# Another slot plan for the first batch of an attention and mixture kernel: maxima, stores, ropes, resident weights

## The chip, the cores and the metric

One core of a Trainium2 chip runs the whole program. The metric is the device time of one execution in microseconds, as the median of several runs. Smaller is better. The compute engines are TensorE (PE in the rows), VectorE (DVE), ScalarE (ACT) and GpSimd (POOL); SyncE (SP) only issues transfers here.

## The reference, cut to what matters

For four batches of 512 tokens with 512 channels:

```python
xn = layernorm(x)
q = rope(rms_norm(xn, q_norm_w))            # 16 heads of 32
k = rope(rms_norm(ctx, k_norm_w)); v = ctx  # 4 heads of 32, each for 4 query heads
x = x + (causal softmax(q k / sqrt(32)) v) @ w_out.T
xt = layernorm(x)
probs = softmax(xt @ w_router)              # 128 experts, the 4 largest kept
basis = silu(xt @ w_gate) * (xt @ w_up)     # 8 units of 256
x = x + sum over the kept experts of coeff * (mix of basis) @ w_down
      + (silu(xt @ shared_w_gate) * (xt @ shared_w_up)) @ shared_w_down
```

## The kernel before

**Precision.** Products are made from high and low parts: a copy into the rounded type is the high half, the original minus it the low half. A product of weights is three matmuls: high by high, high by low, low by high. So every weight chunk in use has to be split first: the high half on ScalarE (`weights_high`, L931), the low one on VectorE (`weights_low`, L1260) for three of the four row blocks and on GpSimd (L889) for the fourth. The router's weights and `w_down` stay in SBUF and are split once: `resident_high` on ScalarE (L933) and `resident_low` on VectorE (L1263), in slot 36. `mixture_table` (L1244), six small instructions on VectorE, stands in slot 32.

**Slots.** There is one time axis of slots, from -40 to 247. Each engine's program is a loop over the slots; in each it asks a fixed list of questions ("is there a tile to turn here?") and emits what is due, with semaphore waits for its inputs. So tables of slot numbers at the top of the file set each engine's order. An engine never overtakes in its own list, and neither does SyncE's queue of transfers.

**Attention.** A batch is cut in two halves of 256 queries; a half has five tiles: tile 0 (5, 10, ...) the keys, the other four the queries of one key head each. A tile is roped (tiles 0 to 2 on VectorE, the others on GpSimd, first part in its slot, rest in the next), turned by TensorE (L1443), copied out as a high half by ScalarE (`turned_high`, L945) and a low half by VectorE (L1181), and then stacked by DMAs into `k_st` or `q_st`, three for each query head (L679). Tile 5 goes through DRAM: it is stored by two DMAs (L649), waited for, and loaded back by three for each of two pairs of heads (L669). The two halves of a turned tile lie in `turned_h` and `turned_l`, which have two places each, by even and odd tile: tile 6 has to wait until tile 4's copies have read theirs. One span u is a key head in a half; u 0 to 3 is the first half of the first batch, 4 to 7 the second. A span is scored in eight matmuls (L1483), each with a row maximum on VectorE (L1203) and a sum of exponentials on ScalarE (L965). In spans 0 to 3 these exponentials are themselves turned (L1494, out of the bank by L981 on ScalarE). From span 4 on the row maxima are split (L1212, L1214), turned (`maxima_turn`, L1463), copied (`maxima_out`, L957) and sent to `q_st` by two DMAs (L687), and the scores are made a second time, transposed (L1507), with their exponential (L983). Values follow (L1522), and the output's high and low halves (L988, L855).

**Short banks.** Three PSUM banks serve scores, turns, maxima, inverses, router products and x turns in rotation, in the order in which `short_products` lists them; each product waits for the reader of the third before it.

**Mixture.** From slot 32 on (`START`) a token pair each 24 slots: projection and residual (slots 32 and 33 for the first), x turns (35 and 37, L1531), router (38 and 39, L1542), then units of two 512-wide products (from 40, L1607), and the shared and down products. Chunk 0 (`w_out`) is used in slot 32, chunk 1 in 40, chunk 2 in 44, chunk 3 in 46; `SPLIT` puts their high halves 3 and 2 slots before, the low ones 2 and 1. The loads of chunks 0 to 2 and of the resident weights are issued in the first 15 us.

Of the kernel before, what the change touches and what calls it, by code (L numbers as in the profile page):

```python
# [16 lines left out]
LEAD = dict(inverse=-1, spread=2, second_pass=4, inverse_turn=5, values=(9, None), high=0)  # L17

FIRST_TILES = dict(
    rope=(-34, -32, -20, -12, -7, 6, 9, 16, 23, 27), turn=(-17, -13, -8, -1, 6, 12, 15, 21, 27, 34),  # L20
    stack=((), (), (), (), (7,) * 4, (13,) * 2, (16,) * 4, (22,) * 4, (28,) * 4, (35,) * 4))
# [9 lines left out]
THROUGH_DRAM = (5,)  # L31
ROPE_DVE = (0, 1, 2)
# [39 lines left out]
def attention_and_mixture_kernel(nc, x, ctx_in, q_norm_w, k_norm_w, w_out, w_router, w_units, w_down,  # L72
# [48 lines left out]
    with common:  # L121
# [437 lines left out]
        def short_products(s):  # L559
# [11 lines left out]
            if (u := of_later_span(s, "maxima")) is not None:  # L571
                found.append(("maxima", u - KV))
# [60 lines left out]
        def sync_engine(e):  # L633
# [12 lines left out]
            def store_turned(n):  # L646
                for i, (part, made) in enumerate(((turned_h, s_th), (turned_l, s_tl))):
                    e.wait_ge(made, n + 1)
                    e.dma_start(turned_copy[n, i].rearrange("d j q -> j d q"), f32(part[:, n % 2, :])).then_inc(s_stored[n % 2][i], 16)  # L649

            def stack_keys(n, i):
# [7 lines left out]
                if not through_dram(n):  # L659
                    e.wait_ge(s_tl, n + 1)  # L660
                    for head in range(2):
                        for row, part in rows:
                            e.dma_start(f32(k_st[row:row + D, c % KR + head, h * Q:(h + 1) * Q]),
                                        f32((turned_h, turned_l)[part][(j + head) * D:(j + head + 1) * D, n % 2, :])
# [7 lines left out]
            def stack_queries(n, j):  # L672
# [5 lines left out]
                for row, part in ((D, turned_h), (2 * D, turned_h), (0, turned_l)):  # L678
                    e.dma_start(f32(q_st[row:row + D, u % QR, j, :]),  # L679
                                f32(part[j * D:(j + 1) * D, n % 2, :])).then_inc(s_q[u % QR][j], 16)  # L680
# [247 lines left out]
        def scalar_engine(e):  # L928
# [4 lines left out]
            def resident_high():  # L933
                e.wait_ge(s_rt, 16)
                e.activation(rt_w[:, :, 0:NE], rt_raw[:, :, NE:2 * NE], ACT.Copy).then_inc(s_rth, 1)
                e.wait_ge(s_wd, 16)
                for k in range(KD):
                    e.activation(wd_h[:, k, :], wd_raw[:, k, :], ACT.Copy).then_inc(s_wdh, 1)

            def turned_high(n):  # L940
                e.wait_ge(s_turn, n + 1)
                if n - 2 > U0:
                    for s, v in turned_read(n - 2):
                        e.wait_ge(s, v)
                e.activation(turned_h[:, n % 2, :], short("turn", n)[:, 0:Q], ACT.Copy).then_inc(s_th, 1)  # L945
# [104 lines left out]
            for s in slots:  # L1050
                for u in attended_before(s):
# [13 lines left out]
                if s == START[0] + 4:  # L1065
                    resident_high()
# [4 lines left out]
                if (u := of_later_span(s, "maxima")) is not None:  # L1071
# [676 lines left out]
```

## Time and profile before

| | |
|---|---|
| median of 3 runs | 821.03 us (819.33 to 822.58) |
| profiled execution, its own time | 823.38 us |
| its span, first to last instruction | 821.6 us |
| mean granted TensorE clock | 0.979 |
| busy: TensorE / VectorE / ScalarE / GpSimd | 94 / 79 / 70 / 65 % |

The page divides the span in 40 slices; TensorE is under 90% busy in the first six of them and at 90% or more from the seventh on, except the last. Its clock is below full in the third, fourth and fifth. Times in the rows are from the start of the span.

### The profile page before, as it was taken

Reading aid. Unit: us, or ns where it says so; the run is one execution under the profiler, and the core shown is the slowest. Engines: PE = TensorE matmul, PEld = TensorE weight load, DVE = VectorE, ACT = ScalarE, POOL = GpSimd, SP = SyncE. Lnnn points to the kernel's source line nnn. Section 1 sums busy time; section 2 is a strip of 40 time slices with the busy share of each in tenths; the row PEclk is TensorE's granted clock in tenths of the full one; section 3 lists DMA queues with packets and bytes.
Section 4 is the critical chain, followed back from the end, with each engine's and each line's share of the span. In section 5 each row is a group of like instructions: output and inputs, shape, how many; then the busy total and the mean of one; then the engine's idle time right before and its main releaser. Section 6 shows DMA issues by size and latency. Waiting matters only on the chain. (4 is left out here: it accounts for less than half of the span.)

```text
span 821.6 us, 15292 instructions
## 1 busy us (share of the span) xinstructions
PE 771.2 (94%) x4180; PEld 613.0 (75%) x4180; DVE 649.0 (79%) x1635; ACT 576.9 (70%) x1413; POOL 531.3 (65%) x685
## 2 busy tenths in 40 slices
PE   2768689999999999999999999999999999999998
PEld 2645467787778778787778788877778887788876
DVE  6656787888898787888798796888788887688774
ACT  3867877787778677787778677787777775654542
POOL 5546669876577858877477868867465615652561
PEclk9957899999999999999999999999999999999999
DMA  8321225554555445754545445554545345444550
GB/s 294 112 66 34 81 82 174 165 165 149 182 170 173 129 144 178 239 180 135 197 160 164 149 131 181 174 167 156 185 154 177 129 131 197 161 155 156 199 183 26
DMA packets 57053, 127.03 MB, mean 155 GB/s; under 512 B 10921, under 2 KB 28041, under 8 KB 56969
## 3 DMA queue, kind: packets, MB, share of 16 engines
q1 hardware_dynamic: 56968, 126.04, 46.5%
q8 instruction: 36, 0.59, 0.3%
q14 instruction: 49, 0.39, 0.2%
HBM read 107.55 MB, written 4.46 MB: 136 GB/s over the span
## 5 line engine op out<-in xcount | busy, mean ns | idle before, releaser
L1607 PE MATMUL u<-w_h,t_h 128*128 128x512 f32 x640 | 258.1, 403 | 4.3 <-issue 1.9
L1607 PE MATMUL u<-w_l,t_h 128*128 128x512 f32 x640 | 250.4, 391 | 0.0
L1607 PE MATMUL u<-w_h,t_l 128*128 128x512 f32 x640 | 250.3, 391 | 0.0
L1260 DVE TENSOR_TENSOR w_l<-w_raw,w_h 128x512 fp32r<-128x512 f32 x288 | 244.1, 875 | 0.2 <-ACT w_h L931 0.2
L931 ACT ACTIVATE w_h<-w_raw 128x512 fp32r<-128x512 f32 x384 | 219.0, 621 | 11.8 <-DMA w_raw<-in_w_units 11.7
L889 POOL TENSOR_TENSOR w_l<-w_raw,w_h 128x512 fp32r<-128x512 f32 x96 | 138.8, 1445 | 101.8 <-ACT w_h L931 101.6
L965 ACT ACTIVATE scores<-scores,mx 128x384 f32<-128x384 f32 (+1 forms) x224 | 128.8, 575 | 76.0 <-DVE mx L1203 74.6
L897 POOL TENSOR_TENSOR macc<-macc,gb 128x256 f32<-128x256 f32 x112 | 106.2, 952 | 63.9 <-DVE gb L1363 63.5
L1203 DVE CUSTOM_DVE_ANT_0 scores<-s,mask_qk 128x384 f32<-128x384 f32 (+1 forms) x224 | 112.5, 503 | 42.1 <-PE s L1483 41.1
L1607 PEld LDWEIGHTS u<-w_h,t_h 128*128 128x128 f32 x640 | 120.6, 188 | 30.5 <-issue 7.0
L1607 PEld LDWEIGHTS u<-w_h,t_l 128*128 128x128 f32 x640 | 120.1, 188 | 26.9
L1607 PEld LDWEIGHTS u<-w_l,t_h 128*128 128x128 f32 x640 | 120.8, 189 | 19.9
L1483 PE MATMUL s<-k_st,q_st 96*128 96x384 f32 (+1 forms) x248 | 89.5, 373 | 6.6 <-DMA q_st<-turned_l 3.4
L1342 DVE SCALAR_TENSOR_TENSOR th<-th,u 128x256 f32<-128x256 f32 x160 | 66.5, 416 | 36.0 <-ACT th L1030 34.7
L983 ACT ACTIVATE pr<-pair 128x1024 f32<-128x1024 f32 x88 | 77.6, 882 | 20.7 <-PE pair L1507 20.5
L1030 ACT ACTIVATE th<-u 128x256 f32<-128x256 f32 x160 | 60.1, 376 | 36.9 <-PE u L1607 36.5
L872 POOL TENSOR_SCALAR_AFFINE_SELECT pr<-pr 128x512 f32<-128x512 f32 x56 | 46.1, 824 | 36.7 <-ACT pr L983 36.7
L1363 DVE SCALAR_TENSOR_TENSOR gb<-th,wt,u 128x256 f32<-128x256 f32 x112 | 53.9, 481 | 16.0
L1483 PEld LDWEIGHTS s<-k_st,q_st 96*128 96x128 f32 x248 | 49.4, 204 | 19.8 <-issue 11.5
L1507 PE MATMUL pair<-q_st,k_st 98*128 98x512 f32 x148 | 52.5, 422 | 0.9 <-ACT pr L983 0.9
L965 ACT ACTIVATION_READ_ACCUMULATOR scores<-scores,mx 128x1 f32 x224 | 42.5, 190 | 0.0
L1522 PE MATMUL o_bank<-pr,ct 128*32 128x256 f32 (+1 forms) x768 | 42.5, 362 | 0.0
(150 smaller groups left out, 1188.1 us busy)
## 6 DMA issues: line engine op xcount, KB each, us to landing
w_raw<-in_w_units SPq DMA_DIRECT2D x160, 512.0 KB, 4.2
w_raw<-in_w_out_t SPq DMA_DIRECT2D x16, 512.0 KB, 4.7
w_raw<-in_shared_w_down SPq DMA_DIRECT2D x16, 512.0 KB, 4.6
q_st<-turned_h SPq DMA_DIRECT2D x232, 32.0 KB, 2.8
out<-x SPq DMA_DIRECT2D x16, 256.0 KB, 2.1
q_st<-turned_l SPq DMA_DIRECT2D x116, 32.0 KB, 2.6
x<-in_x SPq DMA_DIRECT2D x3, 1024.0 KB, 8.8
k_st<-turned_h SPq DMA_DIRECT2D x48, 32.0 KB, 2.8
```

Source lines behind the costliest of these rows:

```text
L889: e.tensor_tensor(w_l[:, i % WR, k, :], w_raw[:, i % WR, k, :], f32(w_h[:, i % WR, k, :]), ALU.subtract).then_inc(s_wlp, 1)
L897: e.tensor_tensor(total, total, gb[:, adds_before(w, g) % 2, :], ALU.add).then_inc(s_acc, 1)
L931: e.activation(w_h[:, i % WR, k, :], w_raw[:, i % WR, k, :], ACT.Copy).then_inc(s_wh, 1)
L965: e.activation(s, s, ACT.Exp, bias=mx[:, u % 2, t, j:j + 1], scale=-1.0, accum_out=sums[:, u % 2, t, j:j + 1]).then_inc(s_sum, 1)
L983: e.activation(pr[:, n % PR, 0:width], pair[:, 0:width], ACT.Exp, scale=-1.0).then_inc(s_ex, 1)
L1030: e.activation(th[:, n % 2, :], u_bank[filler_no[f] % 2][:, 0:I], ACT.Tanh, scale=0.5).then_inc(s_tanh, 1)
L1203: e.tensor_tensor_reduce(masked_scores(u, m), scores_bank(i)[:, 0:width], mask_qk[:, T - width:T], 1.0, 3e38, ALU.add, ALU.min, mx[:, u % ...
L1260: e.tensor_tensor(w_l[:, i % WR, k, :], w_raw[:, i % WR, k, :], f32(w_h[:, i % WR, k, :]), ALU.subtract).then_inc(s_wl, 1)
L1342: e.scalar_tensor_tensor(th[:, n % 2, :], th[:, n % 2, :], 1.0, up, ALU.add, ALU.mult).then_inc(s_ga, 1)
L1363: e.scalar_tensor_tensor(to, th[:, n % 2, :], scale, gate_v, ALU.mult, ALU.mult).then_inc(s_gb, 1)
L1483: e.matmul(scores_bank(i)[:, 0:w], q_st[0:MAXROW, u % QR, j, t * P:(t + 1) * P], k_st[0:MAXROW, (b * KV + kv) % KR, 0:w], start=True, stop ...
L1607: last = e.matmul(u_bank[n % 2][:], t[:, k, cols], ww[:, i % WR, k, :], start=(k == 0 and m == 0), stop=(k == KC - 1 and m == 2))
```

## The change

It moves work between slots in the first batch and changes who does part of it:

- `FIRST_TILES`: the ropes of tiles 6 to 9 go from slots 9, 16, 23, 27 to 8, 14, 19, 24; the second moments from slot 7 to 5, the query scale from 9 to 7, the spreading of the inverse by one slot.
- Stacking: the fourth query head of tile 4 is copied in slot 13, behind the stores of tile 5 (slot 12); tile 6's first head (16) goes ahead of the first key pair of tile 5 (17); then two heads of tile 6 (18), the second key pair and the last head (19).
- `OWN_PLACE`: tile 6's halves lie in the first columns of `t_h` and `t_l`, the buffers of the turned x, which are first used in slot 35; the first x turn's copy waits for tile 6's copies.
- For spans 4 to 7 the turn of the maxima and its copy stand ahead of the tile turn in their slot, on TensorE, on ScalarE and in the order of the short banks (`maxima_in`).
- The resident weights are split wholly by VectorE, one of six steps in each of slots 12, 13, 14, 15, 16 and 18, the copies with `tensor_copy`; the table of the mixture is in slot 19.
- `FIRST_SPLIT`: chunk 0's halves in slots 15 to 18, chunk 1's in 29 to 31, chunk 2's in 37 to 39.

```diff
-LEAD = dict(inverse=-1, spread=2, second_pass=4, inverse_turn=5, values=(9, None), high=0)
+LEAD = dict(inverse=-1, spread=1, second_pass=4, inverse_turn=5, values=(9, None), high=0)
 FIRST_TILES = dict(
-    rope=(-34, -32, -20, -12, -7, 6, 9, 16, 23, 27), turn=(-17, -13, -8, -1, 6, 12, 15, 21, 27, 34),
-    stack=((), (), (), (), (7,) * 4, (13,) * 2, (16,) * 4, (22,) * 4, (28,) * 4, (35,) * 4))
+    rope=(-34, -32, -20, -12, -7, 6, 8, 14, 19, 24), turn=(-17, -13, -8, -1, 6, 12, 15, 21, 27, 34),
+    stack=((), (), (), (), (7, 7, 7, 13), (17, 19), (16, 18, 18, 19), (22,) * 4, (28,) * 4, (35,) * 4))
...
+OWN_PLACE = 6
...
-PREP = dict(key_squares=(-39, 4, -29, -10), key_scale=(-36, 5, -26, -7), query_scale=(-35, 9, -23, -6))
+PREP = dict(key_squares=(-39, 4, -29, -10), key_scale=(-36, 5, -26, -7), query_scale=(-35, 7, -23, -6))
 SPLIT = dict(high=(3, 2), low=(2, 1))
-MOMENTS = (-39, -38, 4, 7, -32, -27, -13, -9)
+FIRST_SPLIT = dict(high=((15, 17), (29, 30), (37, 38)), low=((16, 18), (30, 31), (38, 39)))
+RESIDENT, MIX_TABLE = (12, 13, 14, 15, 16, 18), 19
+MOMENTS = (-39, -38, 4, 5, -32, -27, -13, -9)
...
+        def maxima_in(s, first):
+            u = of_later_span(s, "maxima")
+            return u if u is not None and (u < H * KV) == first else None
...
         def splits(s, name):
-            return [(i, k) for i, at in enumerate(chunk_slot) for ks, ahead in zip(((0, 1), (2, 3)), SPLIT[name])
-                    if s == at - ahead for k in ks]
+            found = []
+            for i, at in enumerate(chunk_slot):
+                early = FIRST_SPLIT[name]
+                places = early[i] if i < len(early) else [at - ahead for ahead in SPLIT[name]]
+                found += [(i, k) for ks, place in zip(((0, 1), (2, 3)), places) if s == place for k in ks]
+            return found
...
+        def turned(n):
+            return (t_h[:, 0, 0:Q], t_l[:, 0, 0:Q]) if n == OWN_PLACE else (turned_h[:, n % 2, :], turned_l[:, n % 2, :])
...
             found += [("scores", u * G * TH + m) for u, m in first_pass_tiles(s)[:1] if not apart(u * G * TH + m)]
+            if (u := maxima_in(s, first=True)) is not None:
+                found.append(("maxima", u - KV))
             for n in tiles_in(s, "turn"):
...
-            def resident_high():
-                e.wait_ge(s_rt, 16)
-                e.activation(rt_w[:, :, 0:NE], rt_raw[:, :, NE:2 * NE], ACT.Copy).then_inc(s_rth, 1)
-                e.wait_ge(s_wd, 16)
-                for k in range(KD):
-                    e.activation(wd_h[:, k, :], wd_raw[:, k, :], ACT.Copy).then_inc(s_wdh, 1)
...
             def turned_high(n):
                 e.wait_ge(s_turn, n + 1)
-                if n - 2 > U0:
-                    for s, v in turned_read(n - 2):
+                for m in [m for m in range(U0 + 1, n) if m % 2 == n % 2 and OWN_PLACE not in (m, n)][-1:]:
+                    for s, v in turned_read(m):
                         e.wait_ge(s, v)
-                e.activation(turned_h[:, n % 2, :], short("turn", n)[:, 0:Q], ACT.Copy).then_inc(s_th, 1)
+                e.activation(turned(n)[0], short("turn", n)[:, 0:Q], ACT.Copy).then_inc(s_th, 1)
...
+                elif g == 0:
+                    for s, v in turned_read(OWN_PLACE):
+                        e.wait_ge(s, v)
...
-            def resident_low():
-                e.wait_ge(s_rth, 1)
-                e.tensor_tensor(rt_w[:, :, NE:2 * NE], rt_raw[:, :, NE:2 * NE], f32(rt_w[:, :, 0:NE]), ALU.subtract).then_inc(s_rtl, 1)
-                for k in range(KD):
+            def resident_weights(step):
+                if step == 0:
+                    e.wait_ge(s_rt, 16)
+                    e.tensor_copy(rt_w[:, :, 0:NE], rt_raw[:, :, NE:2 * NE]).then_inc(s_rth, 1)
+                elif step == 1:
+                    e.wait_ge(s_rth, 1)
+                    e.tensor_tensor(rt_w[:, :, NE:2 * NE], rt_raw[:, :, NE:2 * NE], f32(rt_w[:, :, 0:NE]), ALU.subtract
+                                    ).then_inc(s_rtl, 1)
+                elif step < 2 + KD:
+                    k = step - 2
+                    e.wait_ge(s_wd, 16)
+                    e.tensor_copy(wd_h[:, k, :], wd_raw[:, k, :]).then_inc(s_wdh, 1)
+                else:
+                    k = step - 2 - KD
                     e.wait_ge(s_wdh, k + 1)
-                    e.tensor_tensor(wd_l[:, k, :], wd_raw[:, k, :], f32(wd_h[:, k, :]), ALU.subtract
-                                    ).then_inc(s_wdl, 1)
+                    e.tensor_tensor(wd_l[:, k, :], wd_raw[:, k, :], f32(wd_h[:, k, :]), ALU.subtract).then_inc(s_wdl, 1)
...
-                if s == START[0]:
-                    mixture_table()
-                if s == START[0] + 4:
-                    resident_low()
...
+                if s in RESIDENT:
+                    resident_weights(RESIDENT.index(s))
+                if s == MIX_TABLE:
+                    mixture_table()
```

In `store_turned`, `stack_keys`, `stack_queries` and `turned_low` the operands come from `turned(n)`; the loops of ScalarE and TensorE ask `maxima_in(s, first=True)` at the head of the slot, or behind the first scores, and `first=False` where they asked before.

## Rows read from the trace of the kernel before

**Rows 1.** Windows: stretch, its length, busy us (instructions) by engine, clock, DMA share, GB/s.
```profile
36.00:53.80 17.80, 10.32 (x65) 7.84 (x61) 7.27 (x38) 11.74 (x40) 11.27 (x22) 0.69 0.26 68
...
117.00:821.60 704.60, 694.24 (x3775) 556.66 (x3773) 568.86 (x1375) 499.38 (x1213) 466.54 (x564) 1.00 0.49 161
```

**Rows 2.** TensorE's waits from 50 to 120 us: us in total, times, longest.
```profile
PE s L1531 <- DVE mx L1203: 3.8, 2, 2.0
PE s L1483 <- DMA q_st<-turned_l: 3.4, 2, 3.1
PE s L1443 <- POOL r_b L849: 1.9, 2, 1.0
PE u L1607 <- DVE w_l L1260: 1.4, 2, 0.8
...
PE s L1463 <- DVE mhl L1214: 1.0, 1, 1.0
PE pair L1507 <- ACT pr L983: 0.9, 1, 0.9
...
PE u L1591 <- POOL o_l L855: 0.5, 1, 0.5
```

**Rows 3.** Timeline, TensorE: start us, us, instruction, idle before it and releaser.
```profile
53.82 0.66 PE L1483 MATMUL s<-k_st,q_st 96*128 96x384 f32 x1 [3.06 <-DMA q_st<-turned_l]
...
85.03 0.63 PE L1531 MATMUL s<-ident,xn 128*128 128x128 f32 x4 [1.79 <-DVE mx L1203]
...
91.61 1.08 PE L1531 MATMUL s<-ident,xn 128*128 128x128 f32 x4 [1.98 <-DVE mx L1203]
```

**Rows 4.** Timeline, the queue of SyncE.
```profile
34.83 1.24 SPq L679 DMA_DIRECT2D q_st<-turned_h  x2
...
43.72 0.64 SPq L649 DMA_DIRECT2D turned_copy<-turned_h  x1
...
47.16 3.13 SPq L669 DMA_DIRECT2D k_st<-turned_copy  x6
50.39 1.22 SPq L679 DMA_DIRECT2D q_st<-turned_h  x2
```

**Rows 5.** Timeline, VectorE; first its group of low halves from the page.
```profile
L1260 DVE TENSOR_TENSOR w_l<-w_raw,w_h 128x512 fp32r<-128x512 f32 x288 | 244.1, 875 | 0.2 <-ACT w_h L931 0.2
...
40.35 0.42 DVE L1181 TENSOR_TENSOR turned_l<-s,turned_h 128x256 fp32r<-128x256 f32 x1 [1.27 <-ACT turned_h L945]
...
46.50 0.28 DVE L1203 CUSTOM_DVE_ANT_0 early<-u,mask_qk 128x128 f32<-128x128 f32 x1
...
54.52 0.56 DVE L1203 CUSTOM_DVE_ANT_0 scores<-s,mask_qk 128x384 f32<-128x384 f32 x1 [2.37 <-PE s L1483]
...
73.11 0.78 DVE L1246 TENSOR_TENSOR amp<-amp 128x16 f32<-128x16 f32 x1
...
74.71 0.29 DVE L1256 TENSOR_SCALAR mixs<-amp_s,es 128x8 f32<-128x8 f32 x1
...
88.61 0.85 DVE L1265 TENSOR_TENSOR rt_w<-rt_raw,rt_w 128x512 fp32r<-128x512 f32 x1 [0.99 <-ACT rt_w L935]
89.38 1.28 DVE L1268 TENSOR_TENSOR wd_l<-wd_raw,wd_h 128x512 fp32r<-128x512 f32 x2
...
99.44 1.23 DVE L1212 TENSOR_SCALAR mhl<-mx 128x8 fp32r<-128x8 f32 x1
```

**Rows 6.** Timeline, ScalarE.
```profile
45.07 0.38 ACT L945 ACTIVATE turned_h<-s 128x256 fp32r<-128x256 f32 x1 [1.52 <-DMA q_st<-turned_l]
...
48.31 1.00 ACT L981 ACTIVATE pr<-pair 128x1024 f32<-128x1024 f32 x1
...
68.59 1.13 ACT L931 ACTIVATE w_h<-w_raw 128x512 fp32r<-128x512 f32 x2
```

**Rows 7.** Timeline, GpSimd.
```profile
42.59 0.72 POOL L849 TENSOR_TENSOR r_b<-r_b 128x256 f32<-128x256 f32 x1
...
99.37 1.27 POOL L889 TENSOR_TENSOR w_l<-w_raw,w_h 128x512 fp32r<-128x512 f32 x1 [2.59 <-ACT w_h L931]
```

More of the change, by code:

```diff
@@ L570, in short_products @@
             found += [("scores", u * G * TH + m) for u, m in first_pass_tiles(s)[1:] if not apart(u * G * TH + m)]
-            if (u := of_later_span(s, "maxima")) is not None:
+            if (u := maxima_in(s, first=False)) is not None:
                 found.append(("maxima", u - KV))
@@ L646, in store_turned @@
             def store_turned(n):
-                for i, (part, made) in enumerate(((turned_h, s_th), (turned_l, s_tl))):
+                for i, (part, made) in enumerate(zip(turned(n), (s_th, s_tl))):
                     e.wait_ge(made, n + 1)
-                    e.dma_start(turned_copy[n, i].rearrange("d j q -> j d q"), f32(part[:, n % 2, :])).then_inc(s_stored[n % 2][i], 16)
+                    e.dma_start(turned_copy[n, i].rearrange("d j q -> j d q"), f32(part)).then_inc(s_stored[n % 2][i], 16)
             def stack_keys(n, i):
@@ L663, in stack_keys @@
                             e.dma_start(f32(k_st[row:row + D, c % KR + head, h * Q:(h + 1) * Q]),
-                                        f32((turned_h, turned_l)[part][(j + head) * D:(j + head + 1) * D, n % 2, :])
+                                        f32(turned(n)[part][(j + head) * D:(j + head + 1) * D, :])
                                         ).then_inc(s_k[c // 2 % (KR // 2)][h], 16)
@@ L677, in stack_queries @@
                 e.wait_ge(s_tl, n + 1)
-                for row, part in ((D, turned_h), (2 * D, turned_h), (0, turned_l)):
+                for row, part in ((D, 0), (2 * D, 0), (0, 1)):
                     e.dma_start(f32(q_st[row:row + D, u % QR, j, :]),
-                                f32(part[j * D:(j + 1) * D, n % 2, :])).then_inc(s_q[u % QR][j], 16)
+                                f32(turned(n)[part][j * D:(j + 1) * D, :])).then_inc(s_q[u % QR][j], 16)
             def rows(u):
@@ L1050, in scalar_engine @@
             for s in slots:
+                if (u := maxima_in(s, first=True)) is not None:
+                    maxima_out(u)
                 for u in attended_before(s):
@@ L1064, in scalar_engine @@
                     x_high(g)
-                if s == START[0] + 4:
-                    resident_high()
                 if (p := routing(s, "choose")) is not None:
@@ L1070, in scalar_engine @@
                     row_sum(u, m)
-                if (u := of_later_span(s, "maxima")) is not None:
+                if (u := maxima_in(s, first=False)) is not None:
                     maxima_out(u)
@@ L1180, in turned_low @@
                 e.wait_ge(s_th, n + 1)
-                e.tensor_tensor(turned_l[:, n % 2, :], short("turn", n)[:, 0:Q], f32(turned_h[:, n % 2, :]), ALU.subtract
+                high, low = turned(n)
+                e.tensor_tensor(low, short("turn", n)[:, 0:Q], f32(high), ALU.subtract
                                 ).then_inc(s_tl, 1)
@@ L1389, in vector_engine @@
                     evict[fillers[s - 1][0]](fillers[s - 1])
-                if s == START[0]:
-                    mixture_table()
-                if s == START[0] + 4:
-                    resident_low()
                 for u, m in first_pass_tiles(s)[1:]:
@@ L1652, in tensor_engine @@
                     pass_a(u, m)
+                if (u := maxima_in(s, first=True)) is not None:
+                    maxima_turn(u)
                 for n in tiles_in(s, "turn"):
@@ L1660, in tensor_engine @@
                     pass_a(u, m)
-                if (u := of_later_span(s, "maxima")) is not None:
+                if (u := maxima_in(s, first=False)) is not None:
                     maxima_turn(u)
```

## The prediction

> **What bounds the kernel now.** The page's busy shares put TensorE first of the engines. The windows by stretch, read next, show where it is not busy: from 117 us to the end it is busy 694.2 of 704.6 us, with the clock granted at 1.00, while between 36 and 53.8 us it is busy 10.3 of 17.8, at a mean clock of 0.69, so that part of this stretch runs at the lower of the two levels, 1.2 GHz instead of 2.4 [rows 1]. Every engine works through a list whose order is fixed by slots. What TensorE gains before 117 us is therefore kept: the rest is its own work and moves forward as a block. What the change does in slots 5 to 45 is to be read from who releases TensorE there. The table of its waits from 50 to 120 us names them: VectorE's row maxima 3.8 us, a query DMA 3.4, the rope tiles of GpSimd 1.9, low weight halves 1.4, the split maxima 1.0, the second exponential 0.9, the low half of the attention output 0.5 [rows 2]. The timeline gives the place of each.
>
> **The clock of the slots.** By order and shape of the instructions, TensorE's 53.82 us in [rows 3] is slot 21, the first scores of the second half (span 4); 85.03 is the first x turn in slot 35, 91.61 the second x turn in slot 37. 72 us is slot 32, 101 us slot 40 and 117 us slot 45.
>
> **Part 1, the stores and copies.** SyncE issues tile 4's twelve copies from 34.83 on, then makes the two stores of tile 5 from 43.72 on, waits for the landing, loads the keys from 47.16 and starts tile 6's queries only at 50.39 [rows 4]; TensorE stands at 53.82 for them, 3.06 us [rows 3]. In the new order three of tile 4's copies go behind the store. One head is three issues, about 1.9 us (six took 3.13 [rows 4]), so the store goes out near 41.8, and the moved head by 44.9. Tile 6's first head needs its low half, which was there some 0.8 us after ScalarE's high half began at 45.07. That had waited 1.52 us for tile 4's copies to leave the buffer [rows 6]; in a place of its own tile 6 does not, and I put its low half at 45.2. It is issued by 47.0, the two key heads by 48.8. Before, the first head's last issue ended near 50.39 + 1.9 = 52.3 and TensorE went on at 53.82, 1.5 later [rows 3, 4]; so all is there at about 50.3, with 1 us of doubt. The DMA wait is gone. Cover for the later heads is thin: the fourth is issued by 56 us and needed near 60.
>
> What is late next? The resident weights, chunk 0 and the table of the mixture are put in just this stretch. **VectorE** in slots 12 to 18 gets three copies, three subtractions and chunk 0's three subtractions, and in slot 19 the table. Subtractions of this size take 1.28 us for two [rows 5], so I take 0.6 apiece. A copy of this shape on VectorE isn't in the trace; half of that, 0.3, is one end, and 0.6 plus the wait below is the other, and I take 0.6, since the operand is as long. Before slot 17's row maximum stand seven of these nine, 4.2 us. The engine was idle there for some 3.3 us between the tile-5 low half at 40.35 and that maximum at 46.50 [rows 5], of which tile 6's shorter wait takes back about 0.6. So the maximum comes at 48.3 to 48.5. **ScalarE** waits for it, then has the two high halves that are new in slot 17, 1.13 us for two, and only then the sum and the exponential that began at 48.31 [rows 6]: now 50.6. TensorE's next turning of probabilities needs it out of its bank. Before, TensorE stood at slot 21 from 53.82 - 3.06 = 50.76 on [rows 3], 2.45 us after that exponential's start; so it comes to slot 21 at about 53.1. Also the table, 1.9 us from 73.11 to 75.00 [rows 5], now stands before the last maximum of slot 20. VectorE's first maximum of the second half, 54.52 before [rows 5], comes at 53.5 to 54.2. I book 1.0 us of the 3.4; bounds are -1.5 (each of nine operations 0.3 dearer than taken) and +3.4 (all hidden).
>
> On GpSimd's side the trace shows a VectorE instruction of 8 elements a partition that took 1.23 us from 99.44; it ended when the subtraction on GpSimd that had begun at 99.37 and lasted 1.27 us ended [rows 5, 7]. So a neighbour on GpSimd can hold a small one-source operation for its whole length. Tile 7's rope now runs in slots 14 and 15, beside those copies. It speaks against moving copies to VectorE, and rival (c) has its price. The Trainium skill states it as a rule (SBUF — State Buffer, section "SBUF: two separate sides"): a VectorE operation in a two-port mode, or one with two SBUF inputs, and a GpSimd operation exclude each other for a whole instruction. The row at 99.44 agrees.
>
> **Part 2, ropes sooner.** GpSimd made tile 6 last at 42.59 to 43.31 [rows 7], behind an output half that waits for the values of span 0. With the second moments in slot 5, the scales in slot 7 and the first part in slot 8 it ends near 41.6. That only feeds tile 6's turn, which stands before the chain counted above: no gain of its own. Tiles 8 and 9 are made in slots 19 and 24 instead of 23 and 27, where GpSimd had been idle. Tile 8's turn then doesn't wait, about half of the 1.9 us for ropes, 0.9 [rows 2]. The other half is tile 10's, in the second batch, whose chain starts at the first residual and isn't touched. The maxima of span 4 wait for their split, which stands on VectorE behind tile 8's low half, and move with it: this is the same 0.9 us, not a second one. GpSimd is then also free when the output half for the first projection is due: 0.5 us [rows 2], against nothing if ScalarE's half comes no sooner; I take it whole. Sum 1.4.
>
> **Part 3, the maxima sooner.** The maxima now stand ahead of the turn in the order of the three short banks too, so that each short product waits for another reader. In slot 35 the x turn waited for the maximum of its third predecessor; this now is a low half, up to 1.79 us earlier [rows 3]. But the scores right behind it (6.3) take over the same wait, by which they start at most 0.5 us sooner, and behind them tile 10's rope holds. Gain zero, bound 0.5. In slots 28, 34 and 40 the rows of the maxima go out to the queue 1 to 3 us sooner; no wait for them is in the table, so I book nothing. In slot 40 the maxima wait for the logits in the turn's place (1.1 us, which stays).
>
> **Part 4, the resident weights out of slot 36.** VectorE spent 88.61 to about 90.6 on three subtractions [rows 5], and behind them came the maximum that the second x turn awaited until 91.61, 1.98 us [rows 3]. Without them the maximum comes 2 us sooner, and the x turn starts where TensorE had begun to wait, at 91.61 - 1.98 = 89.6. It had run at 1.2 GHz, too: 1.08 us for four transposes, where the first x turn took 0.63 [rows 3]. Behind it ScalarE is busy nearly without a gap until 101 us, so the shift is passed on. I book 2.3 of 2.0 to 2.6.
>
> **Part 5, chunks 1 and 2 sooner.** Chunk 2's halves leave slots 41 to 43 for 37 to 39, where chunk 1's had been, and chunk 1's take chunk 0's old slots. The loads had long landed. So slots 29 to 31 and 37 to 39 have the same amount as before, and 41 to 43 have less by three subtractions on VectorE. TensorE's two waits for low weights, 1.4 us, and the wait on an exponential, 0.9 us [rows 2], whose maximum stood behind them, go: 2.3 us. From below it is bounded by 1.0, if the next chunk (issued to the queue in slot 34, used in 46) or SyncE's long line of copies is late next.
>
> **Sum.** 1.0 + 1.4 + 0 + 2.3 + 2.3 = 7.0 us. The profiled run took 823.38 us for its span of 821.6, the median is 821.03; so the span would be 814.6, such a profiled run 816.4, and against the median the forecast is 814.0.
>
> **Rivals.**
> (a) Everything early is hidden and the clock helps. If copies cost 0.3 and the chain in slots 12 to 20 stays under TensorE's own slow work, all 3.4 us of the DMA wait are won, 2.4 more; and with fewer gaps before 66 us the clock may not fall there, for which I put 1.0 of TensorE's work that runs slowly today. 7.0 + 3.4 = 10.4, so 810.6. For it: VectorE is busy only 7.3 of 17.8 us between 36 and 53.8 [rows 1]. Against it: the operations stand in front of maxima, in the same queue.
> (b) The early chain costs its lower bound, -1.5 in place of 1.0, and part 5 gives 1.0 in place of 2.3: 7.0 - 2.5 - 1.3 = 3.2, so 817.8. For it: ScalarE has 11.7 of 17.8 us there already [rows 1] and gets two more. This is also the case in which the DMA order does not help at all, since TensorE is late anyway.
> (c) Slower: VectorE and GpSimd hold each other. The nine operations and the table's first, ten, each wait a full neighbour as the one at 99.44 did. That instruction's excess is at least 1.1 us over one of a few hundred ns, and 10 x 1.1 = 11, all on the chain of slots 12 to 20: 821.0 - 7.0 + 11 = 825.0. It turns the change slower from 0.7 us apiece. Against it: the 288 low halves of the whole run, beside a GpSimd in all states, took 875 ns in the mean against 640 for those at 89.38, an excess of 0.24 [rows 5].
>
> **How the numbers follow.** The forecast has 0.46, with 811.5 to 816.5 as its own range; (a) 0.18, (b) 0.26, (c) 0.10. The range of 809 to 820 leaves out most of (c) and the best of (a). Half a per cent, 4.1 us, is about what a measurement of this kernel can tell. Faster by more is under 816.9: nearly all of the forecast and (a) and a little of (b), 0.66. Within it: most of (b) and some of (c), 0.26. Slower: 0.08.
>
> **What the profile after would show.** Part 1: no wait for a query DMA at slot 21, keys issued before 49 us; and TensorE at slot 21 at about 53, with ScalarE's sum of slot 18 behind two high halves. If slot 21 begins near 51, (a) is right; at 54 or later, (b) or (c). VectorE's copies: 0.3 or 0.6 us, and above 1 us beside GpSimd for (c). Part 2: no rope wait at tile 8. Part 4: the second x turn 1.5 to 2 us sooner after tile 10's turn. Part 5: no low-weight waits in slot 44. TensorE should reach its unbroken stretch near 110 us instead of 117; the busy 694 us behind it should stay. What would make all of it wrong is a fall of the clock in a place where it now is 1.00, or a wait in slots 44 to 50 that today hides behind those that go.

## The result and the profile after

The changed kernel takes 815.57 us in the median (814.18 to 816.52, six runs), the kernel before 820.86 beside it: a ratio of 0.9937, 95% interval 0.9921 to 0.9952, so 5.2 us less. A second comparison gave 0.9950 (experiment 1). The profiled execution took 816.52 us for a span of 814.8. That of before lay 2.5 us above its median and this one 0.95 above its own, so the two traces show 6.9 us of difference where the medians show 5.2. The other 1.7 us come from which executions were profiled, and not from the change.

TensorE is at 94% of the span as before, VectorE up from 79 to 80. Windows by stretch (stretch, its length, busy us and instructions of TensorE, its weight loads, VectorE, ScalarE, GpSimd; clock, DMA share, GB/s):

```profile
36.00:53.80 17.80, 10.21 (x56) 7.57 (x54) 13.17 (x42) 12.41 (x38) 16.21 (x24) 0.67 0.26 72
66.00:82.00 16.00, 14.06 (x64) 9.98 (x56) 10.28 (x30) 12.81 (x29) 7.18 (x14) 0.79 0.26 83
82.00:100.00 18.00, 14.10 (x82) 9.43 (x83) 12.50 (x35) 15.18 (x38) 12.48 (x23) 0.81 0.15 43
117.00:814.80 697.80, 687.55 (x3743) 551.23 (x3741) 565.07 (x1361) 493.03 (x1198) 460.61 (x558) 1.00 0.49 162
```

The late stretch is as full as it was: 687.6 of 697.8 us, against the row in [rows 1]. What changed lies ahead of it. In 36 to 53.8 us VectorE went from 7.3 busy us to 13.2 and GpSimd from 11.3 to 16.2, and TensorE has about the same (10.2 against 10.3). Its waits from 50 to 120 us, to be read against [rows 2]:

```profile
PE pair L1518 <- ACT pr L991: 4.6, 2, 3.1
PE s L1507 <- DVE mx L1217: 3.7, 3, 2.0
...
PE u L1615 <- POOL o_l L872: 0.4, 1, 0.4
```

The 3.4 us for a query DMA, the rope waits, the 3.8 at the x turns and the 1.4 for low weights are no longer in the table. (In the trace of experiment 1, the same kernel at a fuller clock, one rope wait of 1.3 us is there again.) In the place of the first stands a wait on ScalarE's exponential of up to 3.1 us, and one on VectorE's maximum of 2.0. TensorE's timeline gives the places:

```profile
51.02 1.09 PE L1518 MATMUL pair<-ident,early 128*128 128x128 f32 x4 [3.07 <-ACT pr L991]
52.11 0.52 PE L1507 MATMUL s<-k_st,q_st 96*128 96x384 f32 x1
55.48 1.10 PE L1507 MATMUL s<-k_st,q_st 96*128 96x384 f32 x2 [1.99 <-DVE mx L1217]
...
80.18 0.66 PE L1555 MATMUL s<-ident,xn 128*128 128x128 f32 x4
82.22 0.47 PE L1507 MATMUL s<-k_st,q_st 96*128 96x512 f32 x1 [1.39 <-DVE mx L1217]
...
86.80 0.63 PE L1555 MATMUL s<-ident,xn 128*128 128x128 f32 x4
```

Slot 21 (96x384 at 52.11) has no wait of its own any more and begins 1.7 us sooner than the 53.82 of [rows 3], but two waits of 3.07 and 1.99 us stand around it. The x turns start at 80.18 and 86.80 without a wait (85.03 and 91.61 in [rows 3]).

Two traces need not start alike. The third of TensorE's early groups of transposes stands ahead of all that was changed, and so serves as a mark; first before, then after:

```profile
19.01 1.94 PE L1455 MATMUL u<-ident,r 128*96 128x128 f32 x8 [2.67 <-DVE r L1177]
18.80 1.94 PE L1479 MATMUL u<-ident,r 128*96 128x128 f32 x8 [2.67 <-DVE r L1190]
```

### The profile page after: what moved, and what is told of

It is laid out like the page before. It is cut to its first block and busy times, and to the rows that moved or that the text cites. A ratio compares the mean times of both kernels' runs of the same rounds, so it can differ in the third digit from the quotient of the medians.

```text
span 814.8 us, 15292 instructions
## 1 busy us (share of the span) xinstructions
PE 768.0 (94%) x4180; PEld 610.7 (75%) x4180; DVE 651.2 (80%) x1638; ACT 576.1 (71%) x1410; POOL 531.6 (65%) x685
```

## The experiments

All times below as "us under before" are (1 - ratio) times the median of the kernel before in the same session: 820.43 (experiments 1 to 4), 819.88 (5 to 8), 820.55 (9 to 12).

**1. The changed kernel again.** No edit.

> The changed kernel once more, as the yardstick for its neighbours on the same chip. All theories: 5 to 6 us under the kernel before (ratio 0.993).

Ratio 0.9950, 0.9934 to 0.9966: 4.1 us under before. Its profiled run has the clock at 1.00 from 82 to 100 us where the first one had 0.81:

```profile
82.00:100.00 18.00, 12.54 (x80) 9.16 (x73) 13.59 (x38) 15.53 (x39) 12.84 (x24) 1.00 0.13 35
```

Nearly the same instructions, another clock, and a span of 812.0 instead of 814.8. Of the 2.8 us, 1.0 was there before the clocks differed: the mark stands at 17.83 instead of 18.80, and from it to the third score of the second half both traces take 36.7 us.

```profile
17.83 1.94 PE L1479 MATMUL u<-ident,r 128*96 128x128 f32 x8 [2.68 <-DVE r L1190]
```

So a single trace says where an engine waits, but its total is no measure of a variant to 2 us.

**2. The order alone.** Parts 1 to 3 stay; the resident weights go back to ScalarE and slot 36, the table to 32, all chunks to their old slots.

```diff
-FIRST_SPLIT = dict(high=((15, 17), (29, 30), (37, 38)), low=((16, 18), (30, 31), (38, 39)))
-RESIDENT, MIX_TABLE = (12, 13, 14, 15, 16, 18), 19
+FIRST_SPLIT = dict(high=(), low=())
+RESIDENT, MIX_TABLE = (12, 13, 14, 15, 16, 18), 32
...
+                if s == START[0] + 4:
+                    resident_high()
...
+                if s == START[0] + 4:
+                    for step in (1, 4, 5):
+                        resident_weights(step)
```

The first of these stands on ScalarE, the three subtractions on VectorE; `RESIDENT` itself is no longer asked.

> The changed kernel's stores, copies, ropes, own place and maxima, but resident weights, table and chunk splits where they were before. Theory 1 (the weights' work in slots 12 to 19 takes the place of the DMA wait): without that work the 3.4 us of the wait are really won, and 1.4 at tile 8 and the first projection; 4 to 5 us faster than before, slot 21's third score near 52.5 us. Rival 2 (something else than that work is late next, so the new order of copies brings nothing): 1 to 2 us faster.

0.9945 (0.9929 to 0.9962), 4.5 us under before, as expected. That is as much as the whole change gives. Slot 21 begins at 49.96, 3.9 us sooner than before, but not without a wait: with VectorE and ScalarE relieved, the keys' loads come last, and they are there close to the 50.3 us at which the prediction had put them.

```profile
49.96 0.42 PE L1517 MATMUL s<-k_st,q_st 96*128 96x384 f32 x1 [1.54 <-DMA k_st<-turned_copy]
```

From 36 to 120 us TensorE waits 5.1 us for stacked keys and queries here. So the new order moves SyncE's queue forward, and in the changed kernel the early work of the other engines hides what is left of it.

**3. The weights alone.** Parts 4 and 5 stay; tiles, stores, ropes and maxima are as before.

```diff
-OWN_PLACE = 6
+OWN_PLACE = None
...
-            return u if u is not None and (u < H * KV) == first else None
+            return u if u is not None and (u < 0) == first else None
```
(and the old lists of ropes, stacks, moments, scale and spread)

> The kernel before with the resident weights, the table and the chunk splits moved, everything else as before. Theory 1: the early work hides under the old DMA wait at slot 21, and the gains at slots 37 and 44 remain: 4 to 5 us faster. With order_only the sum of the two is 8 to 10 and the changed kernel's 5.3 is less than that sum. Rival 2: the early work costs in both kernels, 2 to 3 us faster, and the two parts add up to 5.3.

0.9978 (0.9964 to 0.9993), 1.8 us, under the 4 to 5 of the first theory and just under the 2 to 3 of the rival. TensorE's timeline around slot 21:

```profile
52.20 0.63 PE L1515 MATMUL pair<-ident,early 128*128 128x128 f32 x4 [3.21 <-ACT pr L991]
53.42 0.66 PE L1504 MATMUL s<-k_st,q_st 96*128 96x384 f32 x1 [0.45 <-DMA q_st<-turned_l]
```

The query DMA of [rows 3], unmoved in this kernel, is still awaited, but for 0.45 us instead of 3.06: TensorE now comes late by itself, held 3.21 us by the exponential. The new chain on VectorE and ScalarE fills the old wait to the brim, but delays nothing behind it: the first projection starts at 72.20, before it was 72.03. With the DMA's wait also removed (the full change) the chain takes its place. So the 1.8 us are what parts 4 and 5 bring with an early chain that costs nothing here.

**4. The order and the chunks, with the resident weights late.** All of the change, but the router's weights and the table in slot 32 and `w_down` in 58 to 61.

```diff
-RESIDENT, MIX_TABLE = (12, 13, 14, 15, 16, 18), 19
+RESIDENT, MIX_TABLE = (32, 32, 58, 59, 60, 61), 32
```

(and the loop that emits the steps, so that two may share a slot)

> The changed kernel with the six steps of the resident weights and the table moved to where VectorE waits: router steps and table in slot 32, w_down's in slots 58 to 61 (it is first needed in slot 66). Chunk 0's halves stay in slots 15 to 18. Theory 1: the VectorE chain of slots 12 to 19 is shorter by some 7 us of work, slot 21 starts 1.5 to 2.5 us sooner, and the total is 7 to 8 us under the kernel before. Rival 3 (ScalarE's two high halves of chunk 0 in slot 17 make the delay, not VectorE's): as the changed kernel, 5 to 6 us.

0.9914 (0.9894 to 0.9933), 7.1 us under before and 3 under the changed kernel in the same session, as the first theory said. VectorE and ScalarE:

```profile
44.53 1.67 DVE L1274 TENSOR_TENSOR w_l<-w_raw,w_h 128x512 fp32r<-128x512 f32 x2
...
52.18 0.56 DVE L1217 CUSTOM_DVE_ANT_0 scores<-s,mask_qk 128x384 f32<-128x384 f32 x1
```
```profile
48.38 1.00 ACT L991 ACTIVATE pr<-pair 128x1024 f32<-128x1024 f32 x1
```

The exponential begins 1.5 us sooner than after's 49.87 and the first maximum of the second half 2.6 sooner than its 54.77. Slot 21 begins at 50.62, 1.5 sooner. TensorE still waits 2.9 us for that exponential (to 49.52), which stands behind chunk 0's high halves as well.

**5 to 7. The three parts of the order, one at a time.** Before, with only the stack lists and `OWN_PLACE`; only the ropes, moments, scale and spread; only `maxima_in`.

```diff
-    stack=(..., (7,) * 4, (13,) * 2, (16,) * 4, ...)
+    stack=(..., (7, 7, 7, 13), (17, 19), (16, 18, 18, 19), ...)     # 5: with OWN_PLACE = 6
...
-    rope=(-34, -32, -20, -12, -7, 6, 9, 16, 23, 27)
+    rope=(-34, -32, -20, -12, -7, 6, 8, 14, 19, 24)                 # 6
...
+            if (u := maxima_in(s, first=True)) is not None:           # 7
+                maxima_turn(u)
```

> The kernel before with the new order of stores and copies and tile 6's own place, nothing else. Theory 1 (the DMA wait at slot 21 was a real 3.4 us): 2 to 3.5 us faster than before, less than the full wait because tile 6's rope still comes at 43.3 us. Rival 2 (only the order together with the ropes does it): within 1 us.

0.9966 (0.9951 to 0.9981), 2.8 us, as expected. No DMA is among TensorE's waits from 36 to 120 us. The ropes (3.4 us) and the maxima at the x turns (3.4) are first in the table now; in the same window of the kernel before they had 3.0 and 3.8, so neither has taken the DMA's place. The wait for low weights, with the chunks where they were before, is half of the 1.4 in [rows 2]:

```profile
PE u L1641 <- DVE w_l L1283: 0.7, 1, 0.7
```

> The kernel before with only the ropes, second moments, query scales and inverse spreads sooner. Theory 1: 1.4 us faster (tile 8's rope wait and the output half for the first projection), the DMA wait stays. Rival 2: nothing, as the shift at slot 27 goes to SyncE's queue.

0.9989 (0.9975 to 1.0002), 0.9 us, which the interval does not hold apart from nothing. The DMA wait that the stores would have removed is there as before:

```profile
PE s L1514 <- DMA q_st<-turned_l: 3.4, 2, 3.0
```

> The kernel before with only the maxima of spans 4 to 7 turned and copied sooner. Theory 1: within 0.5 us of before, since no wait for their rows stood in the table. Rival 4 (the other readers that the bank rotation gives each product cost or save something at the x turns): 1 us or more, either way.

1.0002 (0.9990 to 1.0013): nothing. The table of waits shows that it did act: of two waits at the x turns, 3.8 us in [rows 2], one is left. The time is the same, so what the turn gained was lost behind it, as part 3 of the prediction argued.

```profile
PE s L1562 <- DVE mx L1223: 2.0, 1, 2.0
```

The three add to 2.8 + 0.9 - 0.2 = 3.5 us against 4.5 together. The intervals of the four (about 1.2 us each way) leave open whether together they are worth more.

**8. The order, resident weights late, chunks unmoved.**

```diff
-FIRST_SPLIT = dict(high=((15, 17), (29, 30), (37, 38)), low=((16, 18), (30, 31), (38, 39)))
-RESIDENT, MIX_TABLE = (12, 13, 14, 15, 16, 18), 19
+FIRST_SPLIT = dict(high=(), low=())
+RESIDENT, MIX_TABLE = (32, 32, 58, 59, 60, 61), 32
```

> resident_late with the chunk splits of before (chunk 0 in slots 29 to 31, 1 in 37 to 39, 2 in 41 to 43). Theory 1: part 4's 2.3 us on top of order_only's 4.6, about 813.5, and the chunk moves are worth about 1 us beside resident_late. Rival 3 (chunk 0's halves in slots 15 to 18 cost as much as chunk 2's departure from slots 41 to 43 brings): the same 812.5 as resident_late or less.

0.9936 (0.9919 to 0.9953), 5.3 us, only 0.7 more than the order alone and less than expected. TensorE's table of waits, 36 to 120 us, has a DMA in it: the rows of the maxima, which stand in SyncE's queue behind the copies of the tiles.

```profile
PE pair L1532 <- DMA q_st<-m_t: 2.5, 1, 2.5
```

**9. The order with the chunks moved, resident weights in slot 36.** The edit of experiment 2 without its `FIRST_SPLIT`.

> The changed kernel with only the resident weights and the table put back (slots 36 and 32); the chunk splits stay moved. Theory 1 (the early VectorE work costs as much as slot 36 gives back): within 1 us of the changed kernel, ratio 0.9935 to 0.996. Rival 5 (taking the resident weights out of slot 36 is worth the 2.3 us booked even net of its early cost): 2 us slower than the changed kernel, 0.997.

0.9930 (0.9917 to 0.9943), 5.7 us, 1.2 more than the order alone, which the intervals do not resolve. It lies near the first theory (0.9935 to 0.996) and far from the rival's 0.997.

**10. The order with the resident weights early, chunks unmoved.** The changed kernel with `FIRST_SPLIT = dict(high=(), low=())`.

> The changed kernel with the chunk splits of before (resident weights and table stay in slots 12 to 19). Against order_resident_late (0.9936) it has the VectorE work in slots 12 to 19 instead of 32 and 58 to 61 and nothing else differs. Theory 1: 2 to 3.5 us slower than that, 0.9965 to 0.998. Rival 3 (the early cost is chunk 0's alone): equal to it, 0.9936.

0.9918 (0.9902 to 0.9935), 6.7 us. Both expectations missed: the kernel is not slower than with the resident weights late (experiment 8) but 1.4 us faster, which the intervals do not resolve. The early resident weights by themselves bring 2.2 us over the order alone, about what part 4 booked without any cost. VectorE, ScalarE and TensorE:

```profile
45.26 0.68 DVE L1293 TENSOR_TENSOR wd_l<-wd_raw,wd_h 128x512 fp32r<-128x512 f32 x1
45.86 0.28 DVE L1217 CUSTOM_DVE_ANT_0 early<-u,mask_qk 128x128 f32<-128x128 f32 x1
...
46.41 0.81 DVE L1293 TENSOR_TENSOR wd_l<-wd_raw,wd_h 128x512 fp32r<-128x512 f32 x1
...
51.60 0.56 DVE L1217 CUSTOM_DVE_ANT_0 scores<-s,mask_qk 128x384 f32<-128x384 f32 x1
```
```profile
47.32 1.02 ACT L991 ACTIVATE pr<-pair 128x1024 f32<-128x1024 f32 x1
```
```profile
65.69 1.22 PE L1531 MATMUL pair<-q_st,k_st 98*128 98x512 f32 x2 [1.55 <-DMA q_st<-m_t]
```

The maximum of slot 17 comes at 45.86, the exponential at 47.32 and the first maximum of the second half at 51.60: all sooner than with the resident weights late but chunk 0 moved (experiment 4).

**11. All of the change, resident weights late, and the second half of chunk 0 two slots later** (the low halves of its first half one slot later).

```diff
-FIRST_SPLIT = dict(high=((15, 17), (29, 30), (37, 38)), low=((16, 18), (30, 31), (38, 39)))
-RESIDENT, MIX_TABLE = (12, 13, 14, 15, 16, 18), 19
+FIRST_SPLIT = dict(high=((15, 19), (29, 30), (37, 38)), low=((17, 20), (30, 31), (38, 39)))
+RESIDENT, MIX_TABLE = (32, 32, 58, 59, 60, 61), 32
```

> resident_late with chunk 0's second high halves behind slot 19's exponential instead of ahead of slot 18's, and its low halves in slots 17 and 20. Theory 1 (two high halves on ScalarE stand in the chain of slots 17 to 20 for 1.1 us): about 1 us faster than resident_late, 811.5, if SyncE's queue does not take it. Rival 6 (from resident_late on SyncE's queue of copies is the bound of slots 21 to 31): the same 812.5.

0.9907 (0.9895 to 0.9920), 7.6 us, the fastest of all, though with four runs only and not resolved from experiment 4, so neither theory is decided. The exponential that began at 48.38 there comes at 46.51, 1.9 us sooner than there, and TensorE's third score still waits for a maximum, and its transposed scores for the rows:

```profile
52.92 1.10 PE L1508 MATMUL s<-k_st,q_st 96*128 96x384 f32 x2 [1.85 <-DVE mx L1217]
...
65.85 0.74 PE L1532 MATMUL pair<-q_st,k_st 98*128 98x512 f32 x2 [1.16 <-DMA q_st<-m_t]
```

**12. Tile 7's rope out of the crowded slots.** The changed kernel with that rope in 17 instead of 14, to take GpSimd's two passes away from VectorE's copies.

```diff
-    rope=(-34, -32, -20, -12, -7, 6, 8, 14, 19, 24)
+    rope=(-34, -32, -20, -12, -7, 6, 8, 17, 19, 24)
```

> The changed kernel with tile 7's rope in slots 17 and 18 instead of 14 and 15, so that VectorE's copies in slots 14 and 15 and chunk 0's first low halves have no rope beside them on GpSimd. Theory 1 with contention (each operation beside GpSimd pays 0.2 to 1 us): 1 us faster than the changed kernel in the end and w_l in slot 16 at 1.28 us for two instead of 1.55. Rival 7 (the contention only moves to slots 17 and 18): the same within 0.7 us.

0.9940 (0.9926 to 0.9954), the same as the changed kernel. The contention moved elsewhere, as the rival said: VectorE's low halves of the chunk came down to 1.28 us for two, and `w_down`'s took 1.22 each where 0.69 is usual, the first beside the output's low half (GpSimd, 45.32 to 46.58), the second beside the rope (48.55 to 49.70).

```profile
44.71 1.28 DVE L1274 TENSOR_TENSOR w_l<-w_raw,w_h 128x512 fp32r<-128x512 f32 x2
45.91 1.22 DVE L1293 TENSOR_TENSOR wd_l<-wd_raw,wd_h 128x512 fp32r<-128x512 f32 x1
49.03 1.22 DVE L1293 TENSOR_TENSOR wd_l<-wd_raw,wd_h 128x512 fp32r<-128x512 f32 x1
```

**The kernels with the new order, side by side** (us under before):

| resident weights | chunks unmoved | chunks moved | moved, chunk 0 partly later |
|---|---|---|---|
| slot 36 | 4.5 (exp. 2) | 5.7 (9) | |
| early, 12 to 18 | 6.7 (10) | 5.2 and 4.1 (the change; 1) | |
| late, 32 and 58 to 61 | 5.3 (8) | 7.1 (4) | 7.6 (11) |

Going down the left column, early is worth 2.2 us. Along the top, moved chunks are worth 1.2. Were both free of each other the change would stand at 4.5 + 2.2 + 1.2 = 7.9; it stands at 4.1 to 5.2. So the two together lose some 3 us, and they meet in slots 12 to 19. A rival is that both relieve the same slots 36 to 45, so that the second brings less. The last row speaks against it: slot 36 is free of resident weights there too, and the moved chunks keep their gain (5.3 to 7.1). A fair warning on sizes: each cell is uncertain by about 1.3 us, and the 3 us, a sum over four cells, by about 2.4 (an estimate, the half widths added in squares). Experiment 4 and the changed kernel in its session (0.9894 to 0.9933, 0.9934 to 0.9966) just fail to overlap, 11 is clearly apart from the changed kernel, and 10 and the changed kernel overlap.

The traces say where these are lost, once each is read from the mark of its own trace. Start of three instructions of TensorE, and in brackets the lead over the kernel before, counted from the mark:

| kernel | mark | third score of the second half | first projection |
|---|---|---|---|
| before | 19.01 | 55.69 | 72.03 |
| the change | 18.80 | 55.48 (0.0) | 69.73 (2.1) |
| the change again (1) | 17.83 | 54.50 (0.0) | 68.74 (2.1) |
| order alone (2) | 18.75 | 51.66 (3.8) | 68.60 (3.2) |
| weights alone (3) | 18.88 | 55.83 (-0.3) | 72.20 (-0.3) |
| order and chunks (9) | 18.32 | 51.86 (3.1) | 66.44 (4.9) |
| order, resident weights early (10) | 18.77 | 52.31 (3.1) | 67.03 (4.8) |

With either piece of early work alone TensorE is 3.1 us ahead at the third score; with both, twice over, it is level with the kernel before. At the first projection it is still 2.7 to 2.8 us behind either. So what the two pieces cost each other is lost ahead of slot 32. The last four kernels have one trace each.

## Why the prediction was right, and where not

The time and the sign were forecast rightly, 1.6 us below what was measured: 5.2 us were won of the 7.0 booked. That the profiled run took 816.52 where 816.4 was forecast is luck, as a second one of the same kernel took 813.69. Of the steps, these held and these did not.

**Part 1 was right in mechanism and mis-sized.** SyncE, to be read against [rows 4]:

```profile
39.83 0.65 SPq L666 DMA_DIRECT2D turned_copy<-turned_h  x1
...
44.17 1.14 SPq L696 DMA_DIRECT2D q_st<-t_h  x2
...
45.99 1.52 SPq L686 DMA_DIRECT2D k_st<-turned_copy  x3
```

The first store goes out at 39.83 (said: near 41.8), tile 6's head at 44.17 and the first key pair by 47.5 (said: before 49). The DMA wait is gone, and then what was said to be late next was late: VectorE's maximum of slot 17, ScalarE's exponential behind two high halves, then slot 21, each forecast within 1 us. (Two slips in the working changed little: 46.50 plus 4.2 less the idle 3.3 - 0.6 is 48.0, not 48.3 to 48.5, and nine operations 0.3 dearer each take 1.0 to -1.7, not -1.5.)

```profile
48.34 1.13 ACT L948 ACTIVATE w_h<-w_raw 128x512 fp32r<-128x512 f32 x2
49.87 1.00 ACT L991 ACTIVATE pr<-pair 128x1024 f32<-128x1024 f32 x1
```

The exponential was forecast at 50.6 and came at 49.87; slot 21 at 53.1, and came at 52.11. But the term did not end there. It was booked as "VectorE's first maximum of the second half comes at 53.5 to 54.2", and that comes at 54.77, 0.25 us later than the 54.52 of [rows 5]: the second new wait, 1.99 us before the third score. So the 1.0 us booked measures -0.25 at that point, and -0.5 from the mark, in the trace of experiment 1 as in this one. What lengthened it is on VectorE and GpSimd:

```profile
39.05 0.88 DVE L1281 CAST rt_w<-rt_raw 128x512 fp32r<-128x512 f32 x1
42.37 0.42 DVE L1289 CAST wd_h<-wd_raw 128x512 fp32r<-128x512 f32 x1
...
45.28 1.55 DVE L1274 TENSOR_TENSOR w_l<-w_raw,w_h 128x512 fp32r<-128x512 f32 x2
46.75 0.94 DVE L1293 TENSOR_TENSOR wd_l<-wd_raw,wd_h 128x512 fp32r<-128x512 f32 x1
47.62 0.28 DVE L1217 CUSTOM_DVE_ANT_0 early<-u,mask_qk 128x128 f32<-128x128 f32 x1
...
48.99 0.69 DVE L1274 TENSOR_TENSOR w_l<-w_raw,w_h 128x512 fp32r<-128x512 f32 x1 [0.74 <-ACT w_h L948]
49.60 1.77 DVE L1293 TENSOR_TENSOR wd_l<-wd_raw,wd_h 128x512 fp32r<-128x512 f32 x1
...
52.69 0.85 DVE L1270 TENSOR_SCALAR mixs<-amp_s,es 128x8 f32<-128x8 f32 x1
...
54.77 0.56 DVE L1217 CUSTOM_DVE_ANT_0 scores<-s,mask_qk 128x384 f32<-128x384 f32 x1
```
```profile
49.55 1.27 POOL L906 TENSOR_TENSOR w_l<-w_raw,w_h 128x512 fp32r<-128x512 f32 x1 [0.58 <-ACT w_h L948]
50.77 1.06 POOL L832 TENSOR_TENSOR rw_b<-x,mv 128x256 f32<-128x256 f32 x1
52.79 0.72 POOL L848 TENSOR_TENSOR r_b<-rw_b,csq 128x256 f32<-128x256 f32 x1
```

The copies took 0.42 where nothing held them and 0.88 once, 1.7 us for the three where 1.8 was taken. The subtractions were taken at 0.6 apiece; the last of them took 1.77. It starts at 49.60, when GpSimd has just begun (49.55 to 50.82), and ends 0.55 us after GpSimd's instruction, a little less than a subtraction alone (0.69 at 48.99). Then GpSimd's next, begun at 50.77, takes 1.06 us where the same instruction alone takes 0.61 at 59.73, and ends 0.46 after VectorE's. In these rows the two engines take turns, about a whole instruction each. The last of the table's instructions (52.69, 0.85 us, against 0.29 in [rows 5]) ended with the GpSimd instruction of 52.79 to 53.51. In experiment 10, where chunk 0 is not there, the same two subtractions took 0.68 and 0.81, and from the maximum of slot 17 to the first maximum of the second half passed 5.74 us instead of 7.15. So rival (c) was real in its mechanism and smaller in its price: three instructions of the nine and the table took far longer than alone (0.88 for 0.42, 1.77 for 0.69, 0.85 for 0.29) and some others a little (0.94 for 0.69, 1.55 for two), together some 2.8 us over the times alone, not 11. How much of the 3 us that resident weights and chunk 0 cost each other is this taking of turns and how much is plain queueing of one operation behind another was not separated; experiment 12, meant for it, only moved the turns elsewhere.

**Part 2 held.** The maxima of span 4 are turned at 64.37 instead of 65.88, 1.5 us sooner, of which 0.9 was booked for tile 8. The half microsecond of the output half did not come: 0.4 us is still awaited. At the first projection TensorE stands at 69.73 instead of 72.03, 2.3 us sooner, where parts 1 and 2 had booked 2.4. The sum there is right with both of its terms off, the first too large and the second too small. In the trace of experiment 6, part 2 alone, TensorE gains the same 2.1 us between the third score and the projection; its median is only 0.9 under before, so part of that is lost again behind, or lies within the noise.

**An unbooked term.** From the projection to the first residual the trace is 0.76 us shorter than before; the clock of 66 to 82 us is 0.79, and in the kernel before it was

```profile
66.00:82.00 16.00, 15.26 (x60) 10.40 (x58) 10.57 (x33) 11.70 (x27) 8.47 (x15) 0.68 0.11 29
```

Rival (a) had this term, and the forecast did not. It varies from run to run of one kernel (0.79 here, 0.93 in experiment 1), so its size is nothing to count on.

**Part 3 held,** by the trace (the x turn's 1.79 us turned into 1.39 before the scores right behind it) and by experiment 7.

**Part 4 went slightly under, part 5 was read from one trace.** GpSimd's first norm scale and the second x turn mark part 4: 80.54 to 91.61 before, 11.07 us,

```profile
80.54 0.26 POOL L879 TENSOR_SCALAR ln<-mv 128x1 f32<-128x1 f32 x1 [6.69 <-DVE mv L1242]
```

and after, 77.48 to 86.80, 9.32 us:

```profile
77.48 0.27 POOL L896 TENSOR_SCALAR ln<-mv 128x1 f32<-128x1 f32 x1 [5.57 <-DVE mv L1256]
```

That is 1.75 us for the 2.3 booked, and 2.1 in the trace of experiment 1. From tile 10's turn to the second x turn it was 2.65 us and is 0.82, 1.8 sooner, as forecast.

For part 5, no low-weight wait is left, and the last wait before 115 us ends at 109.79 (116.64 before), where "near 110" was said. TensorE leads by 4.8 us at the second x turn and by 6.8 at the end, but these 2.0 us are no proof of part 5: in the traces of experiments 5 to 7, which do not have it, the lead grows by 3.3, 1.3 and 1.2 over the same stretch, so the profiled run of before was a slow one there. The 1.4 us for low weights booked from it are 0.7, 0.6 and 0.7 in those three and 0.3 in experiment 2, and the wait on the exponential is 0.8 there and still 0.5 after. Worked out from these, an estimate of part 5 is 0.6 to 1.0 us in place of 2.3, at its lower bound or under it.

**The sum.** In the medians the order alone has 4.5 us (booked: the DMA wait's 3.4, and 1.4, 4.8), and the weights add -0.4 to +0.7 on top of it, where 7.0 - 4.8 = 2.2 was forecast. The 2.2 was 4.6 gained in slots 35 to 45 less 2.4 for the early chain. The term that was mis-sized most is the gain: the weights alone (experiment 3), whose early chain delays nothing, bring 1.8 us, 3.0 at the most by the interval, and not 4.6. Part 4 is traced at 1.75 to 2.1 of that, so it is part 5 that came short. The price of the early chain shows in the table above: against the order alone it is 3.8 us at the third score, where 2.4 was booked, and 1.1 at the first projection, since the order alone has by then lost some of its lead in waits for SyncE's copies. It comes of both pieces together: with either one alone there is no price left at the projection. That the forecast came as near as it did is in part errors that cancel: part 1 and part 5 too large, part 2 too small, and the clock not booked.

**What is the next bound.** With the early chain eased, waits for the rows of the maxima come up at 65 us (1.47 us in the order alone, 1.55, 2.5 and 1.16 in experiments 10, 8 and 11). The queue of SyncE in experiment 2:

```profile
61.68 1.98 SPq L696 DMA_DIRECT2D q_st<-turned_h  x2
...
64.82 1.29 SPq L704 DMA_DIRECT2D q_st<-m_t  x2
```

The rows wait their turn behind the copies of a tile, some 0.6 us an issue. The prediction gave this line of copies as its lower bound of part 5; it appears already at the transposed scores of the second half.

## What to carry to other kernels

Work moved into a stretch where an engine looks half idle is paid in the order of the queue, not in its busy share: ask which reduction stands behind it, and price the sum of all that is moved there. Two moves that showed no cost one by one (here the resident weights early, and chunk 0 with them late) cost some 3 us when they share the same few slots, so try each alone and both together before settling. A gap in the busy share of TensorE in a stretch of mixed clock cannot be read from one trace: the same kernel gave spans 2.8 us apart. Nor can a short wait: the 1.4 us for low weights in one trace were 0.3 to 0.7 in four others with the same splits. And compare two traces from a mark ahead of the change, as starts alone differed by 1.0 us.

## What the runs showed of the hardware

- A copy of 128x512 from one f32 buffer into another of the rounded type takes VectorE 0.42 us when nothing holds it, where a subtraction of two such operands takes 0.69 (1.28 for two in a row). The Trainium skill (VectorE: DVE Perf Modes, section "Mode 2×_2P — use both read ports for one tensor") has a copy in SBUF at two results a cycle even in f32, and an operation of two tensors at one; the rows agree in direction.
- Beside GpSimd, the copy took 0.88, a subtraction 1.77, and an instruction of 8 elements a partition 0.85 against 0.29. GpSimd is held as well: 1.06 against 0.61. The Trainium skill (SBUF — State Buffer, section "SBUF: two separate sides") states that a VectorE operation in a two-port mode or with two inputs in SBUF and a GpSimd operation exclude each other for a whole instruction; the rows from 49.55 to 51.83 fit it.
- TensorE's clock from 82 to 100 us was 0.81 in one execution and 1.00 in another of the same kernel, with the engine 14.1 and 12.5 of 18 us busy: the less busy one is that with the full clock, since the same work takes less time. The clock of the stretch before does not settle it: from 66 to 82 these two had 0.79 and 0.93, but experiment 3 had 0.68 and then 1.00, and experiment 9 had 1.00 and then 0.81.
